# Silu as one ScalarE function on groups of tiles, and a new slot table, in a chunked scan with a mixed-in network

## What is computed

```
# layer 1: a state-space scan, then a gate
xz = x @ in_proj.T;  x_inner, z = split(xz)
h = exp(dt * A_mean) * h + dt * B_t * u_t           # per step t, state 8 x 512 x 128
y = rms(scan(silu(conv(x_inner)))) * norm_w * silu(z);  y @ out_proj.T
# layer 2: an MLP with ternary weights, 256 -> 1024 -> 1024 -> 1024 -> 256
h = silu(x @ w1.T * s1) * (x @ w2.T * s2);  h = gelu(h @ h1.T * sh1);  h = gelu(h @ h2.T * sh2);  h @ w3.T * s3
# layer 3: linear attention
q, k, v = split(rms(x) @ w_qkv.T);  w = exp(rms(k));  y = sigmoid(rms(q)) * cumsum(w * v) / cumsum(w)
u, g = split(y @ w_swiglu.T);  x + (u * silu(g)) @ w_out.T
# layer 4: two of eight experts
```

## Time and profile before

| | |
|---|---|
| runs | 5642.22, 5631.48, 5640.24 us; median 5640.24 |
| the profiled execution | 5622.6 us, of which the span shown in the trace is 5620.9 us |
| busy over the span | PE 85%, DVE 70%, POOL 71%, ACT 60% |
| first phase | 0 to about 345 us |
| second phase: eight chunks | 382 to 4378 us |
| second phase: tail | 4378 to 4707 us |
| third phase | 4707 to 5621 us |

### The profile page before, as it was taken

The page is one execution under the profiler, slowest core; times in us unless marked ns, Lnnn a source line. Parts: engine busy times, 40 slices in busy tenths (PEclk is TensorE's granted clock), DMA queues, the critical chain, the costliest instruction groups (busy, mean ns, idle before and its releaser), DMA issues. The chain is left out here.

```text
span 5620.9 us, 68943 instructions
## 1 busy us (share of the span) xinstructions
...
## 2 busy tenths in 40 slices
...
GB/s 89 101 155 257 241 240 218 265 255 245 245 259 250 225 250 248 254 227 240 258 235 246 260 262 221 251 266 236 249 248 260 64 75 54 105 107 108 109 111 112
DMA packets 312933, 1138.41 MB, mean 203 GB/s; under 512 B 69664, under 2 KB 123424, under 8 KB 306720
## 3 DMA queue, kind: packets, MB, share of 16 engines
...
## 5 line engine op out<-in xcount | busy, mean ns | idle before, releaser
L1548 POOL TENSOR_TENSOR s_h<-s_decay,s_h 128x768 f32<-128x768 f32 x2048 | 3707.2, 1847 | 288.6 <-ACT s_decay L1200 256.0
L1586 DVE TENSOR_TENSOR s_h<-s_h,bank 128x1024 f32<-128x1024 f32 x2048 | 2470.1, 1215 | 398.3 <-POOL s_h L1548 211.5
L1200 ACT ACTIVATE s_decay<-s_decay,s_a_neg 128x1536 f32<-128x1536 f32 x1024 | 1605.8, 1568 | 117.2 <-DMA s_decay<-dt_rows 116.4
L832 PE MATMUL bank<-s_h,s_cdiag 128*32 128x512 f32 x8192 | 1262.0, 692 | 7.7 <-ACT s_y L1212 6.8
L1205 ACT ACTIVATE bank<-bank,s_a_neg 128x512 f32<-128x512 f32 x1024 | 672.8, 657 | 759.9 <-PE bank L820 757.1
L806 PE MATMUL bank<-s_vrow,s_brow 9*128 9x512 bf16 x4096 | 846.0, 423 | 268.8 <-DVE s_h L1586 241.5
L1576 DVE TENSOR_TENSOR s_h<-bank,s_h 128x512 f32<-128x512 f32 x1024 | 698.8, 682 | 0.6 <-ACT bank L1205 0.5
L806 PEld LDWEIGHTS bank<-s_vrow,s_brow 9*128 9x128 bf16 x4096 | 208.3, 92 | 1498.9 <-issue 1495.5
L944 PE MATMUL bank<-m_mb,m_w 128*128 128x512 f32 x1024 | 521.2, 638 | 0.9 <-ACT m_mb L1278 0.9
L930 PE MATMUL bank<-m_ma,m_w 128*128 128x512 f32 x1024 | 516.3, 633 | 0.0
L820 PE MATMUL bank<-s_drow,s_unit 3*128 3x512 bf16 x1024 | 432.8, 423 | 78.5 <-DMA s_drow<-dt_parts 49.5
...
## 6 DMA issues: line engine op xcount, KB each, us to landing
s_decay<-dt_rows SPq DMA_DIRECT2D x1024, 768.0 KB, 5.3
m_w<-in_units SPq DMA_DIRECT2D x210, 512.0 KB, 5.1
s_vrow<-v_parts SPq DMA_DIRECT2D x1024, 36.0 KB
s_brow<-b_parts SPq DMA_DIRECT2D x1024, 9.0 KB
...
slots<-in_x_tiles SPq DMA_DIRECT2D x128, 96.0 KB, 4.7
...
```

The costliest lines, as they stand in the source:

```text
L832: mm = pe.matmul(bank[q * 32:(q + 1) * 32, Y0], cdiag[:, hf * LANES + q, at * BLK:(at + 1) * BLK], h[:, t % 2, hf * LANES + q], start=(at ...
L1200: act.activation(decay[:, k % RING], decay[:, k % RING], ACT.Exp, scale=a_neg[:, 1:2]).then_inc(decay_ok, 1)
L1548: pool.tensor_tensor(h[:, t % 2, g * PAIR:(g + 1) * PAIR, DCOLS:], decay[:, k % RING, g % 2 * PAIR:(g % 2 + 1) * PAIR], h[:, (t + 1) % 2, ...
L1586: dve.tensor_tensor(h[:, t % 2, g * PAIR:(g + 1) * PAIR], h[:, t % 2, g * PAIR:(g + 1) * PAIR], bank[:, X0 + n % 2 * PAIR:X0 + (n % 2 + 1) ...
```

## The change

The tanh and DVE's product are replaced by ACT's own Silu, in place and on several tiles with one instruction: all 4 tiles of z (128x2048), the gate's 8 tiles as two groups of 4 (128x2048 each), both of the swiglu (128x1024). In the tail the gate's silus are done tile by tile. The halves `half_nw`, `half_s2` and 0.5 go. The slot table is a new one. The core of the diff:

```diff
-Z_AT = (1, 3, 5, 7)
-XN_AT = (9, 12)
-QK_AT = (14, 15, 17, 19)
-GT_AT = (21, 22, 23, 24)
-O_AT = ((27, 28), (30, 31))
-KT_AT = (32, 34)
-QT_AT = (35, 36)
-XT_AT = (40, 43)
-V_AT = (39, 42)
-GATE_AT = (44, 48, 52, 56, 60, 64, 68, 72)
-UP_AT = (46, 50, 54, 58, 63, 66, 71, 74)
+Z_AT = (0, 2, 4, 6)
+XN_AT = (26, 28)
+QK_AT = (30, 31, 34, 36)
+GT_AT = (14, 15, 16, 18)
+O_AT = ((20, 21), (23, 25))
+KT_AT = (60, 68)
+QT_AT = (64, 70)
+XT_AT = (37, 40)
+V_AT = (72, 74)
+GATE_AT = (41, 43, 45, 47, 48, 53, 55, 57)
+UP_AT = (59, 62, 63, 65, 66, 67, 69, 73)
...
-SWI_AT = (174, 176, 188, 189)
-OUT_AT = (201, 203)
+SWI_AT = (173, 175, 186, 187)
+OUT_AT = (200, 201)
...
-SILU_Z_AT = (4, 5, 8, 10)
-SILU_GATE_AT = (47, 51, 55, 59, 63, 67, 71, 75)
-SILU_SWI_AT = (180, 183)
-ROOT_AT = (16, 0, 103)
-SPREAD_AT = (35, 3, 210)
-ROOT_X_AT = 2
-ROOT_Y_AT = 4
-ROOT_QK_AT = 12
-Y_GATE_AT = (13, 15, 17, 21)
+ROOT_AT = (13, 2, 102)
+SPREAD_AT = (32, 7, 209)
+ROOT_X_AT = 9
+ROOT_Y_AT = 3
+ROOT_QK_AT = 21
+Y_GATE_AT = (10, 11, 13, 14)
...
-NORM_1_AT = {2: (0, 1, 2, 3)}
-X_SQ_AT = {2: (0, 1, 2, 3)}
-TO_UNIT_AT = {2: (0,), 3: (1, 2, 3)}
-Y_SQ_AT = {0: (0,), 1: (1,), 2: (2, 3)}
+NORM_1_AT = {4: (0,), 5: (1,), 6: (2, 3)}
+X_SQ_AT = {6: (0, 1), 7: (2,), 9: (3,)}
+TO_UNIT_AT = {10: (0,), 11: (1, 2), 12: (3,)}
+Y_SQ_AT = {0: (0, 1, 2), 1: (3,)}
...
+SILUS = 4
...
-            def tanh_z(m, i):
-                act.wait_ge(S("z_free"), FIRST + m * TT + i + 1)
-                act.activation(ma[:, KI + i], sz[:, i], ACT.Tanh, scale=0.5).then_inc(S("z_th"), 1)
+            def silu_z(m):
+                act.preload_act_table_set("silu_and_others")
+                act.wait_ge(S("z_free"), FIRST + (m + 1) * TT)
+                act.activation(sz, sz, ACT.Silu).then_inc(S("z_ok"), 1)
...
-            def tanh_gate(m, j):
+            def silu_gate(m, j, n):
+                act.preload_act_table_set("silu_and_others")
                 act.wait_ge(S("g_free"), FIRST + m * KH + j + 1)
-                act.activation(ma[:, j], mb[:, j], ACT.Tanh, scale=0.5).then_inc(S("g_th"), 1)
+                act.activation(mb[:, j + 1 - n:j + 1], mb[:, j + 1 - n:j + 1], ACT.Silu).then_inc(S("g_ok2"), 1)
...
-            def tanh_swi(m, i):
-                act.wait_ge(S("sg_free"), FIRST + m * KD + i + 1)
-                act.activation(qk[:, i], u[:, i], ACT.Tanh, scale=0.5).then_inc(S("sg_th"), 1)
+            def silu_swi(m):
+                act.preload_act_table_set("silu_and_others")
+                act.wait_ge(S("sg_free"), FIRST + (m + 1) * KD)
+                act.activation(u[:, 0:KD], u[:, 0:KD], ACT.Silu).then_inc(S("sg_ok"), 1)
...
-            def silu_z(m, i):
-
-                dve.wait_ge(S("z_th"), FIRST + m * TT + i + 1)
-                dve.scalar_tensor_tensor(out=sz[:, i], in0=ma[:, KI + i], scalar=1.0, in1=sz[:, i],
-                                         op0=ALU.add, op1=ALU.mult).then_inc(S("z_ok"), 1)
```

More of the change, by code:

```diff
@@ L556, in stream_phase @@
         k_ = {n: sb("m_" + n, shape) for n, shape in small.items()}
-        half_s2 = sb("m_half_s2", [P, KH])
-        half_nw = sb("m_half_nw", [P, KI])
         mask = sb("m_mask", [P, RUNS])
@@ L1258, in gated_out @@
                 act.wait_ge(S("gT_ps"), FIRST + m * KI + k + 1)
-                act.activation(gT[:, k], bank[:, k if tail else M0], ACT.Identity, scale=half_nw[:, k:k + 1]
+                act.activation(gT[:, k], bank[:, k if tail else M0], ACT.Identity, scale=k_["norm_w"][:, k:k + 1]
                                ).then_inc(S("gT_ok"), 1)
@@ L1485, in _ @@
                 copy_z(end, i, True)
-                tanh_z(end, i)
+            silu_z(end)
             root_var(end - 1, 1)
@@ L1507, in _ @@
                 copy_gate(end, j, True)
-                tanh_gate(end, j)
+                silu_gate(end, j, 1)
             output_tail(end - 1)
@@ L1564, in _ @@
             dve.memset(carry[:, 1], 0.0).then_inc(set_ok, 1)
-            dve.wait_ge(k_in, 16 * (len(small) - 1))
-            dve.tensor_scalar(half_s2[:], k_["s2"][:], 0.5, None, ALU.mult).then_inc(set_ok, 1)
-            dve.tensor_scalar(half_nw[:], k_["norm_w"][:], 0.5, None, ALU.mult).then_inc(set_ok, 1)
-            dve.wait_ge(set_ok, 6)
             def keep(c, k):
@@ L1624, in add_gated @@
                                   ).then_inc(S("o_add"), 1)
[L1626 to L1629 removed]
             def hidden(m, j, tail):
[L1632 removed]
+                dve.wait_ge(S("g_ok2"), FIRST + m * (KH // SILUS) + (j if tail else j // SILUS) + 1)
                 dve.wait_ge(S("up_ps"), FIRST + m * KH + j + 1)
                 dve.scalar_tensor_tensor(out=ma[:, j], in0=bank[:, j % 2 * 2 + 1 if tail else M0],
[L1635 removed]
+                                         scalar=k_["s2"][:, j:j + 1], in1=mb[:, j], op0=ALU.mult, op1=ALU.mult
                                          ).then_inc(S("hid_ok"), 1)
```

74 lines of the change are left out of this document (28 added, 46 removed).

## The result

The changed kernel takes 5663.06 us (median of 5 runs, 5659.39 to 5665.66), the kernel before 5640.24 (5 runs, 5631.48 to 5642.22). The ratio is 1.0043 with a 95% interval of 1.0028 to 1.0058: slower by 23 us, where I had forecast 68 us less.

A forecast was written before the change was run, and what follows sets the result against it. POOL sets the pace, losing 55 us in chunk 3, three quarters to late decays. Terms 8 - 1 + 3 + 1 = 11 us a chunk, 66 in six, + 4 - 2.5 = 68 us saved: 5572 us, range 5500 to 5640.

The forecast's parts named there:

- Z and the start of the chunk: Silu of z, first 48 us of a chunk: POOL's waits fall from 12.0 to 4 us, 8 us saved.
- Gate and crowd: Gate's group silus, with k, q, v among `up` products: loss goes from 9.2 to 10.2 us, 1 lost.
- The crowd itself: K, q and v among the `up` products on PE, slots 62 to 75: 6.5 us lost a chunk.
- Swiglu: Silu replacing two DVE products: mean loss of about 3.5 us becomes a 0.5 stall, 3 us saved a chunk.
- POOL itself: POOL's own instructions, some slower beside products that read two SBUF tiles: 1 us saved a chunk (0 to 4).
- My better case: VectorE 17 us freer: stalls at first gelus go from 7 to 2 us; 20 us a chunk, 5515; chance 0.12.
- Chunk 1: First mixed chunk, without attention: the gate saves about 5 us, z loses 1, so 4 us saved.
- Tail: Load and group silu, 3.2 us, replace the last tanh of z, 0.63: 2.5 us lost on ACT's chain.
- The drain: Each of eight group loads holds ACT 1.3 us longer: chunk loses 10 us, kernel ends at 5635; chance 0.03.
- the 3.2 us of forgiveness: How late ACT's decay may be before POOL waits, read at one gelu with VectorE on time; bad end 1.0.
- My rival with 1.0 us forgiven: Only 1.0 us of ACT's lateness is forgiven: 2 or 3 us saved a chunk, about 5620; chance 0.22.
- The slower rival: Slots 62 to 75: the crowd becomes a chain, eleven slots lose 26 us, kernel at 5692; chance 0.13.

The follow-up runs named there:

- the two profiles of before: The kernel before in its first profiled execution (5622.6 us) and, unchanged, profiled once more (one run, 5645.51 us).
- alone in the old table: The kernel before with only the swiglu's silu changed (one silu on both tiles, no VectorE product): 5646.46 us, ratio 1.0012.
- the new table with tanh: The change's slot table put into the kernel before, with tanh and VectorE's products kept: 5734.99 us, ratio 1.0159.

## Why the prediction was wrong

I go by the steps of its sum, in us a chunk, from the table of stretches with the mean of the two profiles of before.

- **Z and the start of the chunk: 8 saved, measured 3.0** (18.3 to 15.3 in slots 0 to 39; only 1.0 of it in slots 0 to 23, where the 8 were to come from). The block was costed rightly (9.0 us between two decays), the forgiveness was not: 4.99 us of waits against 2.9 forecast. The second half of the miss is the path behind it. I wrote that VectorE's y gates would be late and that three slots of POOL would cover them. Nothing covers the transposes of y, which now stand at slots 14 to 18, right behind the gates: 1.76, 1.10 and 1.64 us of waits, with the granted clock at 0.68 over 1843 to 1891 us.
- **Gate and crowd: 1 lost, measured 9.3** (slots 40 to 95, 12.0 to 21.3). This is the step that failed, in four parts. Group one cost 4.63, not 2.9, and group two 1.61, not 0.85. Ahead of them stand the root and the scalings of q and k, which the new table moved here and of which I had counted one scaling: waits of 1.42 and 1.75 us at 1947.63 and 1952.97, the second behind a gate product that waited 1.76 us for ACT's copy and then took 3.60 us. The crowd itself is near my figure: slots 60 to 79 cost 8.3 us, 1.6 of them the second group's, which leaves 6.7 against the forecast 6.5. And it did not end where I ended it: slots 80 to 95 lost another 2.5 us, with the granted clock at 0.86 where it had been 0.95, one product there taking 3.78 us.
- **Swiglu: 3 saved, measured 2.8** (5.0 to 2.2). The row that I chose against the rule of the Trainium skill, "SBUF — State Buffer", fits better here, since 0.5 was its figure. But that the term came out is luck. I had a loss of 3.5 before and 0.5 after, and the stretch shows 5.0 and 2.2; the silu's own stall is 2.04 us, and 2.71 alone in the old table. Both ends were too low by about 1.6, and the errors cancel.
- **POOL itself: 1 saved.** Its instructions took 14 us less over the run (3693.0 against 3707.2 us on its line), 2 a chunk. That is inside the stretches above, so it is no term of its own.
- **The gelus.** My better case had them gain from a freer VectorE. Slots 96 to 175 went from 11.1 to 10.8 us, so nearly nothing came.
- **Chunk 1: 4 saved, measured 6 lost** (494.8 against 488.7). The second profile of before has 483.9, so it may be 11.
- **Tail: 2.5 lost, measured 0.3.** The drain that "ScalarE: Activation LUTs" of the Trainium skill speaks of is not there either: a load of 1.28 us from 1861.08, the next function at 1862.38.

The terms of a chunk thus give 3 lost in place of 11 saved. In the better case my sum gives 5519 us and not the 5515 that I wrote; nothing hangs on it.

The common error is the 3.2 us of forgiveness. I read it at one place, with VectorE on time, and thought that it needed VectorE alone. The rows show that it is a lead that has to be there. POOL's wait for a decay sets it back to 0.14 us, a half-step in which ACT has to read a late product gives nothing back (0.13 us at slots 48 to 54 of the changed kernel, against 1.65 and 2.77 at slots 56 and 58), and two blocks within five half-steps draw on the same lead. My rival with 1.0 us forgiven was nearer (5620). In the mean its figure is right: forgiven were 0.5, 0 and 2.2 us, and 0.7 at the swiglu. The 43 us that it is short lie mostly in what neither sum had: the y transposes, the root of q and k, slots 80 to 95 and chunk 1. The sign was open to be seen in the trace of before, where no decay of slots 0 to 88 in chunk 3 has more than 1.94 us of lead. DVE's 25 us less a chunk were taken from an engine that had time, and a block of 7 us on ACT was put where POOL already waited for ACT.

The slower rival had the right side, though its chain is not what decided: the loss is 23 us, not 52, and of the 9.3 us lost from slot 40 on more than half stands ahead of slot 60 and behind slot 80.

What caused the 95 us of the new table with tanh is settled by place (slots 24 to 96), not by cause. No kernel undid the place of the y transposes or of q's and k's root alone, so the share of each is read from the waits and is not tested.
